# Attention on one core: the low halves and the output bias on GpSimd, the two projections spread over two units

## The reference, cut to what is computed

```python
xn = _layernorm(x, axis=-1)
qkv = xn @ w_qkv + b_qkv                    # (8, 512, 384)
q, k, v = ...                               # (8, 16, 512, 8) each
attn = softmax(einsum('bhqd,bhkd->bhqk', q, k) * hd ** (-0.5))
out = einsum('bhqk,bhkd->bhqd', attn, v)    # back to (8, 512, 128)
s = out @ w_proj + b_proj
g = silu(experts(xn))                       # two of eight experts for each token
x = x + s * g
```

## Time and profile before

| what | value |
|---|---|
| three runs | 1035.39, 1027.87, 1030.18 us; median 1030.18 |
| the profiled execution | 1029.66 us, its span 1027.8 us |
| mean granted TensorE clock | 0.924 |
| busy over the span | PE 911.2 us (89%), DVE 823.9 (80%), ACT 596.2 (58%), POOL 550.5 (54%) |
| the costliest groups | line 1735, VectorE's maxima: 512 of 681 ns; line 1346, ScalarE's exponentials: 512 of 594 ns |

### The profile page before, as it was taken

The page is one execution under the profiler, slowest core; times in us unless marked ns, Lnnn a source line. Parts: engine busy times, 40 slices in busy tenths (PEclk is TensorE's granted clock), DMA queues, the critical chain, the costliest instruction groups (busy, mean ns, idle before and its releaser), DMA issues.

```text
span 1027.8 us, 17766 instructions
## 1 busy us (share of the span) xinstructions
PE 911.2 (89%) x5384; PEld 590.5 (57%) x5384; DVE 823.9 (80%) x1875; ACT 596.2 (58%) x1234; POOL 550.5 (54%) x606
## 2 busy tenths in 40 slices
PE   4789999999999999989999954989996999999760
PEld 4544344443444344448888854746654888889760
DVE  7677999999999999615555548699995799999775
ACT  6216888888888888863333326323332777777552
POOL 7322388844444443004555536358785288887660
PEclk9559999999999999999999985699998999999895
DMA  6824656554535543035565744023412467776738
GB/s 200 309 80 146 204 178 214 160 170 131 182 114 177 167 149 104 16 116 192 190 209 179 235 142 123 20 85 110 126 58 88 158 220 219 206 222 212 236 114 250
DMA packets 120208, 164.79 MB, mean 160 GB/s; under 512 B 18321, under 2 KB 81906, under 8 KB 117042
## 3 DMA queue, kind: packets, MB, share of 16 engines
q1 hardware_dynamic: 94290, 109.08, 35.5%
q0 software_dynamic: 17376, 50.38, 14.0%
q10 hardware_dynamic: 8448, 4.20, 1.4%
HBM read 103.92 MB, written 60.06 MB: 160 GB/s over the span
## 4 chain that ended last, share of the span: by engine, by line
PE 50%; POOL 21%; issue 10%; DVE 9%; DMA 5%; ACT 3%; SPq 1%; ACTq 0%; POOLq 0%; DVEq 0%
PE ps L1174 12%; PE ps L1073 12%; POOL slots_x L842 8%; POOL token_y L892 8%; PE ps L1221 5%; PE ps L1079 5%; PE ps L366 3%; PE ps L368 3%; PE ps L367 3%; POOL stage L859 2%; DVE nmax L1735 2%; POOL everstd L866 2%; PE ps L1117 2%; PE ps L1163 1%; DMA stage<-token_y 1%
## 5 line engine op out<-in xcount | busy, mean ns | idle before, releaser
L1735 DVE TENSOR_REDUCE nmax<-ps 128x1 f32<-128x512 f32 x512 | 322.2, 681 | 32.2 <-PE ps L1079 30.9
L1346 ACT ACTIVATE stage<-ps 128x512 f32<-128x512 f32 x512 | 272.9, 594 | 60.9 <-PE ps L1073 56.9
L892 POOL DMA_INDIRECT token_y<-stage,ids_now x156 | 168.9, 1083 | 109.6 <-DVE stage L1794 52.2
L1079 PE MATMUL ps<-stage,stage 32*128 32x512 f32 x512 | 190.2, 507 | 10.8 <-DVE nmax L1735 9.2
L842 POOL DMA_INDIRECT slots_x<-xn,pos x128 | 153.5, 1199 | 40.8 <-issue 39.6
L1073 PE MATMUL ps<-stage,stage 32*128 32x512 f32 x512 | 166.4, 478 | 4.2 <-ACT stage L1346 3.6
L1073 PEld LDWEIGHTS ps<-stage,stage 32*128 32x128 f32 x512 | 66.8, 181 | 144.0 <-ACT stage L1346 126.9
L1174 PE MATMUL ps<-stage,stage 128*32 128x512 f32 x1024 | 136.4, 605 | 0.0
L1221 PE MATMUL ps<-stage,stage 128*128 128x128 f32 (+1 forms) x1092 | 132.2, 277 | 1.2 <-DVE stage L1864 1.0
L1221 PEld LDWEIGHTS ps<-stage,stage 128*128 128x128 f32 (+1 forms) x1092 | 127.6, 194 | 1.8 <-DVE stage L1864 1.4
L366 PE MATMUL ps<-stage,stage 128*128 128x512 f32 (+1 forms) x322 | 122.6, 381 | 4.1 <-ACT stage L1388 3.1
(11 more groups left out here) (244 smaller groups left out, 1492.5 us busy)
## 6 DMA issues: line engine op xcount, KB each, us to landing
stage<-halves_w SPq DMA_DIRECT2D x23, 1024.0 KB, 5.1
stage<-halves_w SPq DMA_DIRECT2D x23, 704.0 KB, 4.6
stage<-slots_x SPq DMA_DIRECT2D x32, 260.0 KB
stage<-q_halves SPq DMA_DIRECT2D x32, 256.0 KB
halves_w<-stage POOLq DMA_DIRECT2D x16, 512.0 KB, 3.2
k_halves<-stage SPq DMA_DIRECT2D x24, 256.0 KB
q_halves<-stage SPq DMA_DIRECT2D x24, 256.0 KB
stage<-k_halves SPq DMA_DIRECT2D x128, 48.0 KB
```

The lines of the kernel that those rows point to most:

```text
L892: pool.indirect_dma_start(out=token_y, out_offset=bass.IndirectOffsetOnAxis(ap=ids_now[:, r, q:q + 1], axis=0), in_=ysb[:, r, q, :], in_of ...
L1079: pe.matmul(ps[:, (0, 1, 7)[bank_of(v, i)], :], head_rows(Qs, g2, j2)[:, t * P:(t + 1) * P], head_rows(Ks, g2, j2), start=True, stop=True) ...
L1346: act.activation(probs[:, t % 2, j, :], ps[:, 2 + bank_of(u, i), :], ACT.Exp, scale=SCALE).then_inc(exp_set, 1)
L1735: dve.tensor_reduce(nmax[:, g % 2, at:at + 1], ps[:, (0, 1, 7)[bank_of(v, i)], :], AX, ALU.max, negate=True).then_inc(max_set, 1)
```

## The change

Four things, all in the attention:

- For sequences 2 to 7, ScalarE writes the whole result of a projection, bias added, into `Lo`, and GpSimd makes both halves from it (`split_half`): a rounding copy into `Hi`, a subtraction in place in `Lo`, which sets `lo_set`. GpSimd does this in `norm_and_scatter`, behind `split_piece(piece)` of the pieces whose u = piece - 4 has g = 2, for the sequence u // 4 + 2. VectorE's `low_half` is left for sequences 0 and 1 alone.
- The keys are projected in unit g = 1 and the queries in unit g = 2, each with two of its three matmuls at t = 2 and the third at t = 3; ScalarE reads either at the end of its unit.
- TensorE's waits for `lo_set` become waits for `hi_set`, ScalarE's copy.
- ScalarE copies the output projection into `attn`, and GpSimd adds the bias there (`add_output_bias`), for the first six sequences behind `split_piece` in g = 1 and for the last two after the loop. The join waits for GpSimd's additions (`pool_side`).

SyncE's program is the same.

```diff
--- before.py
+++ after.py
@@ -311,6 +311,7 @@
         st_mm, exp_set, pv_mm, o_read, oT_mm, onorm_set = (
             sem("st_mm"), sem("exp_set"), sem("pv_mm"), sem("o_read"), sem("oT_mm"), sem("onorm_set"))
         rden_set = sem("rden_set")
+        pool_side = sem("pool_side")
         vT_mm, vT_set, vtp_mm, vaug_set = sem("vT_mm"), sem("vT_set"), sem("vtp_mm"), sem("vaug_set")
         vaug_const = sem("vaug_const")
         onT_mm, onT_set, out_mm, attn_set = sem("onT_mm"), sem("onT_set"), sem("out_mm"), sem("attn_set")
@@ -377,7 +378,8 @@
                 def __init__(self, u):
                     self.main, self.tail = 0 <= u < 32, 1 <= u <= 32
                     self.max, self.load, self.low = 0 <= u + 2 < 32, 0 <= u + 3 < 32, 0 <= u + 1 < 32
-                    self.next = u % GROUPS == 2 and -2 <= u < 24
+                    self.next = u == -2
+                    self.project = u % GROUPS - 1 if 1 <= u < 24 and u % GROUPS in (1, 2) else None
                     self.halves = u % GROUPS == 3 and -1 <= u < 25
                     self.first = u < 1
                     self.even, self.tail_even, self.load_even = (n // GROUPS % 2 for n in (u, u - 1, u + 1))
@@ -799,6 +801,24 @@
                 pool.dma_start(halves_w[L][e, :, :, side * F:(side + 1) * F],
                                raw_halves[:, r, :, 0:F].bitcast(F32)).then_inc(halves_stored[r], 16)
 
+            side = [0]
+
+            def split_half(b, o):
+
+                pool.wait_ge(hi_set, b * 2 + (o + 1))
+                x = Lo[:, 1 - o, :].bitcast(F32)
+                pool.tensor_copy(Hi[:, 1 - o, :], x).then_inc(pool_side, 1)
+                side[0] += 1
+                pool.wait_ge(pool_side, side[0])
+                pool.tensor_tensor(Lo[:, 1 - o, :], x, Hi[:, 1 - o, :].bitcast(F32), ALU.subtract).then_inc(lo_set, 1)
+
+            def add_output_bias(b):
+
+                pool.wait_ge(attn_set, b + 2)
+                pool.tensor_tensor(rows_of(attn, b), rows_of(attn, b), spread(bproj_bc[:, :], 1, [P, QT, D]),
+                                   ALU.add).then_inc(pool_side, 1)
+                side[0] += 1
+
             def outer(m):
 
                 pool.wait_ge(qkv_set, m + 1)
@@ -847,6 +867,16 @@
                             if piece >= 5:
                                 pool.wait_ge(onorm_set, piece - 4)
                             split_piece(piece)
+                            u = piece - 4
+                            if u % GROUPS == 2 and 2 <= u < 24:
+                                split_half(u // GROUPS + 2, 0)
+                                split_half(u // GROUPS + 2, 1)
+                            if u % GROUPS == 1 and u > GROUPS:
+                                add_output_bias(u // GROUPS - 1)
+                if L == 0:
+                    add_output_bias(SEQS - 2)
+                    add_output_bias(SEQS - 1)
+                    pool.wait_ge(pool_side, side[0])
 
             def experts(L):
 
@@ -1091,8 +1121,10 @@
 
 
                         pe.wait_ge(max_set, (u + 2) * 16)
+                        if now.project == 1:
+                            pe.wait_ge(hi_set, b * 2 + 5)
                         if now.halves:
-                            pe.wait_ge(lo_set, b * 2 + 6)
+                            pe.wait_ge(lo_set if u < 0 else hi_set, b * 2 + 6)
                         if g == 0 and now.main:
                             pe.wait_ge(vaug_set, b + 1)
                         if g == 1:
@@ -1120,11 +1152,19 @@
                         pe.wait_ge(onorm_set, u)
                         keep_busy(u)
                         keep_busy(u)
+                    if now.project is not None and t >= 2:
+
+                        if t == 2:
+                            pe.wait_ge(onorm_set, u)
+                        w, (hi, lo) = 1 - now.project, (seq_of(v, b + 2) for v in (xT_hi, xT_lo))
+                        if t == 2:
+                            pe.matmul(ps[:, 6, :], wq_hi[:, w, :], hi, start=True, stop=False)
+                            pe.matmul(ps[:, 6, :], wq_hi[:, w, :], lo, start=False, stop=False)
+                        else:
+                            pe.matmul(ps[:, 6, :], wq_lo[:, w, :], hi, start=False, stop=True).then_inc(proj_mm, 1)
                     if t == 2:
                         if now.next:
 
-                            if now.tail:
-                                pe.wait_ge(onorm_set, u)
                             project(1, b + 2, 6)
                         if g == 0 and now.tail:
                             pe.wait_ge(onorm_set, u)
@@ -1142,7 +1182,7 @@
                                    seq_of(xT_lo, b + 1)).then_inc(vT_mm, 1)
                     if t == 3:
                         if now.next:
-                            pe.wait_ge(lo_set, b * 2 + 5)
+                            pe.wait_ge(lo_set if u < 0 else hi_set, b * 2 + 5)
                             project(0, b + 2, 6)
                         if g == 0 and now.tail:
                             pe.wait_ge(onT_set, b)
@@ -1333,7 +1373,8 @@
                 act.wait_ge(proj_mm, b * 2 + (o + 1))
                 if not (isinstance(b, int) and b < 1):
                     act.wait_ge(halves_out, b * 96)
-                act.activation(Hi[:, 1 - o, :], ps[:, bank, :], ident_f, bias=cols[:, 1 - o:2 - o]).then_inc(hi_set, 1)
+                half = Hi[:, 1 - o, :] if b < 2 else Lo[:, 1 - o, :].bitcast(F32)
+                act.activation(half, ps[:, bank, :], ident_f, bias=cols[:, 1 - o:2 - o]).then_inc(hi_set, 1)
 
             def attend(u, g, b, now):
                 for t in range(4):
@@ -1372,6 +1413,12 @@
                             act.activation(onT, ps[:, 6, :], copy_f).then_inc(onT_set, 1)
                         if (t, j) == (3, 3) and now.next:
                             high_half(b + 2, 1, 6)
+                        if (t, j) == (3, 3) and now.project is not None:
+                            high_half(b + 2, now.project, 6)
+                        if (t, j) == (3, 3) and g == 0 and now.tail:
+                            act.wait_ge(out_mm, b)
+                            act.activation(rows_of(attn, b - 1), ps[:, 6, :].rearrange("p (q d) -> p q d", q=QT),
+                                           copy_f).then_inc(attn_set, 1)
                         if (t, j) == (3, 3) and g == 3 and now.load:
 
                             act.wait_ge(vtp_mm, b + 2)
@@ -1749,9 +1796,9 @@
                             r = (g + 1) % 2
                             dve.tensor_tensor(m_lo[:, r, :], ps[0:16, 6, 0:P], m_hi[:, r, :].bitcast(F32),
                                               ALU.subtract).then_inc(mlo_set, 1)
-                        if (t, j) == (0, 0) and now.halves:
+                        if (t, j) == (0, 0) and now.halves and u < 0:
                             low_half(b + 2, 1, 6)
-                        if (t, j) == (3, 0) and now.next:
+                        if (t, j) == (3, 0) and now.next and u < 0:
                             low_half(b + 2, 0, 6)
                         if (t, j) == (1, 3) and now.tail:
                             dve.wait_ge(oT_mm, u)
@@ -1761,10 +1808,6 @@
                             dve.tensor_tensor(onorm[:, :, 32 * gt:32 * gt + 32].rearrange("p q (j r) -> p q j r", j=4),
                                               turned[:, :, :, 0:HD], spread(rden[:, :, :], 3, [P, QT, 4, HD]),
                                               ALU.mult).then_inc(onorm_set, 1)
-                        if (t, j) == (3, 3) and g == 0 and now.tail:
-                            dve.wait_ge(out_mm, b)
-                            dve.tensor_tensor(rows_of(attn, b - 1), ps[:, 6, :].rearrange("p (q d) -> p q d", q=QT),
-                                              spread(bproj_bc[:, :], 1, [P, QT, D]), ALU.add).then_inc(attn_set, 1)
 
             def experts(L):
                 nch = len(CH[L])
@@ -1936,6 +1979,8 @@
                 def product(b):
                     r = b % 2
                     dve.wait_ge(silu_set[L], b + 1)
+                    if L == 0:
+                        dve.wait_ge(pool_side, 2 * (SEQS - 2) + SEQS)
                     ins = dve.tensor_tensor(sg[:, r, :, :], sg[:, r, :, :], rows_of(attn, b), ALU.mult)
                     if L == 0:
                         link(ins)
```

## The result

The change takes **1061.52 us** in the median of four runs (1059.76 to 1066.41) against 1030.76 of the kernel before in the same session: a ratio of 1.0301, 95% interval 1.0253 to 1.0349. The forecast was 1061. The profiled execution took 1061.98 us, its span 1060.2.

The account below looks back on a forecast made before the run. TensorE and VectorE were taken to set the pace together. 1029.66 + 36.5 (stop) + 2 (clock) - 5 x 1.23 (sequences) - 7 x 0.15 (biases) = 1061 us, range 1050 to 1078.

Parts of the forecast that it names:

- Where it stops, and how long: TensorE stops at the head of unit 5, behind SyncE's wait for GpSimd's halves of sequence 2; 36.5 us.
- The landing: Transfer time of the shift rows after SyncE's last issue near 170.9 us; restart between 173.7 and 175.6, taken as 175.
- The idle time seen: Sign in the profile: an idle stretch of some 37 us on TensorE at the head of unit 5, ended by a transfer.
- The clock: After the stop, 4 us at 1.2 GHz with half the work lost: 2 us, bounds 0 and 6.
- the row of 792 to 797 us: Second experts' matmuls after a pause: clock 0.50, then 1.00 from 798 us; basis for 4 us at 1.2 GHz.
- The gains: Attention units: 1.23 us a sequence for five sequences, and 0.15 us for each of seven output biases.
- a clean pair: Unit g = 3 against the same unit past 24, both with the values' projection: queries' low half priced at 0.32 us.
- The second sequence: GpSimd finishes sequence 3's halves at 192 us, TensorE needs what is queued behind them near 220: no second stop.
- The faster one: Rival: sequence 2's halves are stored before TensorE reaches unit 5, only gains left, 1021 us; chance 0.07.
- no change: Rival: TensorE needs less from behind SyncE's hold, a short stop eats the gains, about 1030 us; chance 0.05.
- the clock that stays low: Rival: 2.4 GHz does not return after unit 5, 115 us more over 27 units, above 1170; chance 0.06.
- Nothing gets shorter: Rival: VectorE is freed but TensorE sets every unit, so the stop alone, 1068 us, inside the range; no separate chance.

Follow-up runs that it names:

- stop_alone: The kernel before with one added wait: SyncE stores sequence 2's halves only after GpSimd's piece 6 has landed; 1071.05 us, ratio 1.0384.
- early: The changed kernel with GpSimd's halves earlier in its queue: sequence 2 ahead of the first scatter, 3 behind piece 6, 4 behind piece 12; 1021.49 us, ratio 0.9904.
- piece4: The changed kernel with sequence 2's halves split on GpSimd behind weight piece 4 instead of piece 6; 1050.34 us, ratio 1.0197.
- warm: The changed kernel with 28 added matmuls on TensorE during the rest of the stop at unit 5; 1063.12 us, ratio 1.0326.
- warm2: The changed kernel with 48 added matmuls on TensorE during the rest of the stop at unit 5; 1058.13 us, ratio 1.0241.
- apart: The kernel before with only the projections moved, keys in g = 1, queries in g = 2; VectorE keeps low halves and bias; 1029.61 us, ratio 1.0003.

## Why the prediction was right, step by step

- **Where it stops, and how long.** The copy at 160.13 us (forecast 159.8), the keys' half at 162.21 (161.8), SyncE's last issue done at 171.05 (170.9), the restart at 173.96 (175), so the stop put TensorE 35.4 us behind (36.5). The first output group of unit 5 is 35.9 us late, as the tiles ahead of it ran at the low clock already. The steps along GpSimd's and SyncE's queues held to half a microsecond. The landing was mis-sized: I took 4.1 us, and it was 2.9. stop_alone makes such a stop by the wait alone, early removes it by the place alone, piece4 shortens it by the two pieces.
- **The idle time seen.** I had said some 37 us of idle TensorE, and the profiled execution shows 25.29. It ran units 0 and 1 at a clock of 0.50 (window 87 to 110 above) and came to unit 5 at 148.7 instead of 138.5 us. That cost nothing, since GpSimd sets the restart; in warm, whose clock was high there, the last matmuls before the stop are at 135 us. The reading of the end was right, that of the gap's start depended on the execution.
- **The clock.** Forecast 2 us (0 to 6), measured 4.0 by the tiles of unit 5 against those of a later unit g = 1, 4.1 by warm2, and 0.5 more ahead of the first output group. The mechanism was right and the size wrong: the row of 792 to 797 us has a short low stretch, while here the clock stayed low for 12 us after the restart. piece4's profiled execution lost 11.1, beyond my upper bound: that end was too low.
- **The gains.** Units g = 2 are 11.09 us (forecast 11.07), g = 3 11.32 (11.32), and g = 1 is 11.21 instead of 11.35: the bias is worth 0.14 (0.15). They add up to 6.7 us behind unit 5 and 0.1 in it (7.2).
- **Why there are gains.** Here the sum was right and its reasons weren't. I had priced a low half at 0.32 us in g = 3, as a clean pair, and had put the 0.91 of g = 2 down to the projection's leaving, the copy and one low half together. By apart a low half costs 0.57 us, and the projections' new place 0.08 us a sequence. The pair wasn't clean. At the end of the unit g = 2 before it TensorE waits 0.41 us for VectorE's maxima already (the weight load at 208.59 us), and within the unit g = 3 only 0.21 and 0.28, where apart has 0.41 twice: part of VectorE's lag was counted in the unit before. What pays is VectorE's relief.
- **The second sequence.** No second stop, as forecast: GpSimd waited for unit normalisation again, first until 184 us, and split sequence 3 from 199 to 203.5. That is later than the 192 that the prediction worked out without such waits, and still far ahead of the need near 220.
- **The rivals.** The faster one was priced at 1021 and never had its condition; early supplies the condition and measures 1021.49. The short stop of "no change" is excluded by TensorE's 25.29 us at the head of unit 5, the clock that stays low by the 289 us at 1.00. "Nothing gets shorter" is excluded by the unit lengths and by early; that TensorE is busy for 287.7 of 289 us would have fitted it.
- **The number.** That the sum came within 1 us is in part luck. The stop was forecast 1.1 us too long and the time behind the attention was 0.6 us shorter than assumed; the clock was priced 2.0 to 2.5 us too low and the gains 0.4 us too high. These errors nearly cancel, and the clock's share alone varied between 0.9 and 11.1 us in the stops that were traced.

## What to carry to other kernels

Before work goes to an engine with room, read when that engine gets to the place in its queue where the code puts it: a mean load of one half hid a lag of 40 us. A late result can also hold up those who don't need it, where an in-order queue carries other things behind it: unit 5 stood for its shift rows, which were queued behind the stores of sequence 2, whose first unit is 8. So look at what stands behind the wait, and who needs that first. The repair was the order alone: the same instructions, put ahead of work that nobody waits for yet, turned 3% slower into 1% faster. Whether issuing the shift rows ahead of the stores in SyncE's queue would have helped as well was not tried.

## What the runs showed of the hardware

The clock of the same work differed between executions. In units 0 and 1 (87 to 110 us) it was 0.50 in the changed kernel, with TensorE busy for 22.22 of 23 us, and 1.00 in early, which computes the same there:

```profile
87.00:110.00 23.00, 22.29 (x147) 8.86 (x151) 21.73 (x40) 18.98 (x39) 2.06 (x4) 1.00 0.69 215
```

Unit 1 then took 15.36 us instead of 11.08. What tips it is open: the profiled executions of piece4 and stop_alone show it too (0.55 in the same window), and warm and warm2 don't; up to there TensorE's instructions are the same in all of these but stop_alone. The stage in front doesn't decide it either: from 38 to 80 us the clock was 0.50 in the changed kernel and in early, and 1.00 in piece4 and warm. A stop inside the kernel may swallow such a loss, as it did here.
